# Mamba stage of a four-layer metaformer: step-size sum and kept columns off VectorE, a new order on four queues, and the conv taps in 8 transfers a pair instead of 18

## The chip, the cores and the metric

One core of a Trainium2 chip runs the whole program in one launch. The metric is the device time of that launch in microseconds. TensorE (PE) multiplies, VectorE (DVE), ScalarE (ACT) and GpSimd (POOL) work on elements, and SyncE (SP) issues the DMAs of this phase. Sixteen DMA engines move the data.

## What is computed

Sixteen images of 24 channels and 56 x 56 pixels go through four layers, each a mixer and a quantized feed-forward network, both with a residual. The change is in the mixer of the second layer alone, a Mamba block. Cut to what matters (`conv2d` is a 3 x 3 depthwise convolution, `conv1d` a causal one of three taps):

```python
xz = in_proj(x)                    # 48 channels to the conv branch, 48 to a gate
u = silu(conv2d(xz[:48]))          # sequence of 3136 pixels
xm, z = m_in_proj(u)               # 48 and 48
xm = silu(conv1d(xm) + b)
dt = softplus(dt_proj(x_proj(xm)[:3]) + dt_b)
B, C = x_proj(xm)[3:19], x_proj(xm)[19:35]
h = exp(dt * A) * h + (dt * xm) * B      # 16 states for each of 48 channels, pixel after pixel
y = sum(h * C) + xm * D
out = out_proj(m_out_proj(y * silu(z)) * silu(xz[48:]))
```

## The kernel before, in words

The phase is `mamba_phase`. The 3136 pixels are cut into 7 *stages* of MT = 448 pixels (8 image rows). There are two kinds of work, in one program order on every engine.

*Items.* An item is one pair of images in one stage; there are 56. Its front end, for item `j + 11` (`front`), multiplies nine shifted copies of the normalized image, the taps, with the folded input and conv weights: `project` (L1248), four matrix products from two tiles, `taps_5` (five taps of 24 channels, 120 partitions) and `taps_4` (96 partitions). `gate_image` (L1353, L1354) applies SiLU. For item `j + 10` (`inner`) follow `convolve` (L1257), `project_z`, `activate_inner` (`xm`), `activate_z` (`zs`), `project_dt`, `project_bc` and the softplus: `step_logs` on ScalarE (L1372 to L1384), `clip` on GpSimd (L1585), `quadratic` on ScalarE (L1395, L1398), `series` on GpSimd (L1590, L1592), and the sum `step_size` on VectorE (L1537). Its results `xm`, `zs`, `dt`, `gs`, `bcs` go to DRAM. The back end of item `j - 10` (`r`) loads `yt` and `gt`, multiplies (L1280), gates on GpSimd (L1597), multiplies (L1287) and stores `res`.

*Steps.* A stage has 6 passes (8 channels of all 16 images on 128 partitions), a pass 8 steps, a step two of the 16 states; 336 steps in all. In step `t` ScalarE makes two decays (`decay`, L1417, two steps ahead, three buffers), VectorE two products (`drive`, L1500) and two scans along the 448 pixels (`scan`, L1513) into one of 8 rows of `h`, GpSimd weighs both rows with `cs` (`weigh`, L1570), and TensorE adds them up in PSUM (`accumulate`, L1301). Once a pass there are `make_u` (L1489) and `times_z` (L1529) on VectorE. Every second step `save` (L1523) copies the last column of four rows of `h` to `kept`, from which the scans of the next stage, 48 steps on, start.

Every queue runs the loop `for j in range(-11, 67)`, `for k in range(6)`, so one item's work is spread over the six slots of six steps (t = 6j + k), each at a slot written by hand, and every engine waits on semaphores in that order. Eleven items pass before the first step: this is the prologue.

SP issues all transfers in that order too. `load_taps(j + 12)` at k = 0 issues 9 taps for each of two images into one of two buffers. `keep_rows` (L1121) stores 48 partitions into a DRAM tensor with dimensions 6 x 8 x 448, `store_bc` (L1143) 64 partitions into `bc_d[2q:2q+2, s]`, two images. At the border of a stage `load_bc(s, g)` (L1167) fills `bs` and `cs` for the next one, with each image repeated on 8 partitions: 8 transfers of 128 x 1792 x 4 bytes. They are issued at steps 48s - 5, - 3, - 1 and + 1, g = 3 right after the taps of that slot. The two sides of a tap transfer are:

```python
tile[m % 2][i][C * row:C * row + C, :]        # 24 partitions x 464
normed[2 * q + i, :, at:at + TAP_N]           # 24 channels x 464
```

Of the kernel before, what the change touches and what calls it, by code (L numbers as in the profile page):

```python
# [12 lines left out]
ALU = mybir.AluOpType  # L13
# [5 lines left out]
C = 24  # L19
# [966 lines left out]
def mamba_phase(nc, w, x, normed, mixed):  # L986
# [4 lines left out]
    with ExitStack() as ctx:  # L991
# [80 lines left out]
         squared, quads, taken, decays) = (buf.sem(n) for n in (  # L1072
             "silu_a", "silu_b", "silu_m", "silu_z", "absed", "relued", "exped", "excess", "lned",
             "bc_copied", "yi_copied", "squared", "quads", "taken", "decays"))
# [16 lines left out]
        with nc.Block() as block:  # L1091
            @block.sync
            def _(sp):
# [106 lines left out]
                for j in range(FIRST, LAST):  # L1200
                    front, inner, r = item(j + LEAD), item(j + LEAD - 1), item(j - LAG)
                    previous, r_done = item(j + LEAD - 2), item(j - LAG - 1)
                    for k in range(6):
# [15 lines left out]
                        if k == 3 and previous is not None:  # L1219
                            store_dt(previous)  # L1220
# [12 lines left out]
            def _(pe):  # L1233
# [71 lines left out]
                for j in range(FIRST, LAST):  # L1305
                    front, inner, r = item(j + LEAD), item(j + LEAD - 1), item(j - LAG)
                    for k in range(6):
                        t = 6 * j + k - 1
                        if k == 0 and front is not None:
                            reached(pe, silu_a, front)  # L1310
                            reached(pe, silu_z, done(front - 1))
                            reached(pe, yi_copied, done(j - LAG))
                            project(front, 0)
                        if k == 1 and front is not None:
                            reached(pe, silu_b, front)
                            reached(pe, relued, done(front - 1))
                            project(front, 1)
# [6 lines left out]
                        if k == 3 and inner is not None:  # L1324
                            reached(pe, taken, done(j - LAG))
                            convolve(inner)
                            project_z(inner)
                        if k == 4 and inner is not None:
                            project_dt(inner)
                            project_bc(inner)  # L1330
                        if k == 4 and r is not None:
                            out_inner(r, j + LEAD - 1)

            @block.scalar
            def _(act):
# [49 lines left out]

                def copy_bc(m):
# [32 lines left out]

                for j in range(FIRST, LAST):  # L1420
                    front, inner, r = item(j + LEAD), item(j + LEAD - 1), item(j - LAG)
                    for k in range(6):
# [3 lines left out]
                        if k == 2 and item(j - LAG - 1) is not None:  # L1426
                            take_result(j - LAG - 1)
# [15 lines left out]
                        if k == 5 and inner is not None:  # L1443
                            quadratic(inner)

            @block.vector
            def _(dve):
# [55 lines left out]
                def scan(t, i):  # L1503
# [12 lines left out]

                def save(t):

                    p, pair = divmod(t, 8)
                    at = p % DB * STATES + 2 * pair - 2  # L1520
                    row = (2 * t - 2) % 8
                    dve.wait_ge(scanned, 2 * t + 2)
                    dve.tensor_copy(kept[:, at:at + 4], h[:, row:row + 4, MT - 1]  # L1523
                                    ).then_inc(saved, 1)
# [15 lines left out]
                for j in range(FIRST, LAST):  # L1540
                    previous = item(j + LEAD - 2)
                    for k in range(6):
                        t = 6 * j + k
                        if 0 <= t < STEPS:
                            if t % 8 == 0:
                                make_u(t // 8)
                            drive(t, 0)
                            drive(t, 1)
                        if t % 2 == 0 and 0 < t <= STEPS:
                            save(t - 1)  # L1550
                        if t % 8 == 3 and 0 <= t // 8 - 1 < PASSES:
                            times_z(t // 8 - 1)
                        if k == 2 and previous is not None:
                            step_size(previous)
                        if 0 <= t < STEPS:
                            scan(t, 0)
                            scan(t, 1)

            @block.gpsimd
            def _(pool):  # L1560
# [26 lines left out]
                def series(m):  # L1587

                    pool.wait_ge(quads, m + 1)
                    pool.tensor_tensor(es[:], quad[:], es[:], ALU.mult).then_inc(sers, 1)  # L1590
                    pool.wait_ge(sers, m + 1)
                    pool.tensor_tensor(es[:], es[:], rv[:], ALU.add).then_inc(summed, 1)  # L1592

# [5 lines left out]
                for j in range(FIRST, LAST):  # L1599
                    inner, previous = item(j + LEAD - 1), item(j + LEAD - 2)  # L1600
                    for k in range(6):
# [3 lines left out]
                        if k == 0 and previous is not None:  # L1605
                            series(previous)
                        if k == 0 and item(j - LAG - 1) is not None:
                            times_gate(j - LAG - 1)
                        if k == 1 and inner is not None:
                            carry(inner)  # L1610
                        if k == 4 and inner is not None:
# [641 lines left out]
```

## Time and profile before

| | |
|---|---|
| median of 3 runs | 4461.85 us (4460.77 to 4468.82) |
| profiled execution | 4458.26 us, its span 4456.6 us |
| granted TensorE clock, mean | 0.931 |
| Mamba phase in the span | 1030 to 2656 us |
| first and last scan | 1204.0 and 2598.9 us |

The profile is one execution. A row of instructions names the line of the kernel, the engine, the operation, the tile written and the tiles read, how often it ran, its busy time and the mean duration of one. Short overlaps of neighbouring instructions are counted twice in busy sums of a group, not in those of an engine.

### The profile page before, as it was taken

How to read it: one execution, taken by the hardware profiler on the slowest of the kernel's cores; microseconds unless marked ns; L12 is line 12 of the kernel's file. 1: busy time of each engine (PE TensorE's matmuls, PEld its weight loads, DVE VectorE, ACT ScalarE, POOL GpSimd, SP SyncE). 2: the span in 40 equal slices, each digit the busy share in tenths (PEclk: the TensorE clock that was granted, in tenths of full speed). 3: DMA queues.
4: the chain of work that ended last, by engine and by line, in shares of the span. 5: the costliest groups of instructions: out<-in, count | busy, mean ns of one | idle time of the engine just before them, and what ended most of it. 6: DMA issues, size and time to landing. Idle time of an engine off the chain costs nothing. (4 is left out here: it accounts for less than half of the span.)

```text
span 4456.6 us, 73149 instructions
## 1 busy us (share of the span) xinstructions
PE 3640.5 (82%) x20680; PEld 2121.9 (48%) x20680; DVE 2888.3 (65%) x4570; ACT 2692.4 (60%) x4664; POOL 1600.1 (36%) x1447
## 2 busy tenths in 40 slices
PE   4899999785677888888876658689999786799956
PEld 2788888442233333333332214344444332799932
DVE  2666666671289989898999937566666665111146
ACT  4555555695666767676765328677777576233346
POOL 0333333101366767676766630045555400000000
PEclk9999999897889989999999979899999988899979
DMA  3000000123536364646544122100000022100012
GB/s 92 19 15 14 14 14 14 35 57 99 152 102 162 116 177 116 172 125 166 152 135 129 52 69 50 39 16 15 15 15 15 9 53 71 34 11 11 11 44 53
DMA packets 203144, 296.59 MB, mean 67 GB/s; under 512 B 68686, under 2 KB 188670, under 8 KB 202242
## 3 DMA queue, kind: packets, MB, share of 16 engines
q1 hardware_dynamic: 193798, 285.57, 24.4%
q10 hardware_dynamic: 9216, 9.65, 0.9%
q8 instruction: 37, 0.61, 0.1%
q14 instruction: 93, 0.76, 0.1%
HBM read 193.01 MB, written 102.03 MB: 66 GB/s over the span
## 5 line engine op out<-in xcount | busy, mean ns | idle before, releaser
L1570 POOL TENSOR_TENSOR mam_hc<-mam_h,mam_cs 128x896 f32<-128x896 f32 x336 | 712.5, 2126 | 333.4 <-DVE mam_h L1513 317.3
L1301 PE MATMUL mam_ps_y<-mam_hc,mam_ident 128*128 128x448 f32 x1344 | 628.4, 595 | 211.0 <-POOL mam_hc L1570 211.0
L1513 DVE TENSOR_TENSOR_SCAN mam_h<-mam_a,mam_kept,mam_dbx 128x448 f32<-128x448 f32 x672 | 729.3, 1123 | 1.2 <-ACT mam_a L1417 1.2
L1417 ACT ACTIVATE mam_a<-mam_ft,mam_a_neg 128x448 f32<-128x448 f32 x672 | 402.1, 656 | 242.4 <-DVE mam_h L1513 241.8
L1944 POOL TENSOR_TENSOR scan_ch<-scan_h,scan_cs 128x392 f32<-128x392 f32 x256 | 344.2, 1360 | 560.8 <-DVE scan_h L1910 560.8
L1301 PEld LDWEIGHTS mam_ps_y<-mam_hc,mam_ident 128*128 128x128 f32 x1344 | 261.3, 204 | 550.0 <-POOL mam_hc L1570 330.7
L1500 DVE TENSOR_TENSOR mam_dbx<-mam_ps_u,mam_bs 128x448 f32<-128x448 f32 x672 | 381.8, 611 | 92.5 <-DMA mam_cs<-dram_bc 91.1
L756 POOL TENSOR_TENSOR att_prob<-att_prob,att_share 128x588 f32<-128x588 f32 x128 | 151.9, 1186 | 452.1 <-DVE att_share L941 452.1
L1910 DVE TENSOR_TENSOR_SCAN scan_h<-scan_turned_in,scan_start 128x392 f32<-128x392 f32 x192 | 256.6, 1356 | 25.6 <-ACT scan_turned_in L1829 24.2
L1784 PE MATMUL scan_ps_merged<-scan_ch,scan_w_merge 128*128 128x392 f32 x512 | 230.6, 532 | 47.8 <-POOL scan_ch L1944 46.0
L2034 PE MATMUL lstm_ps<-lstm_hs,lstm_w_h 128*128 (+1 forms) x1344 | 264.9, 352 | 0.0
L2034 PEld LDWEIGHTS lstm_ps<-lstm_hs,lstm_w_h 128*128 128x128 f32 x1344 | 253.1, 188 | 3.0
L2084 DVE TENSOR_TENSOR lstm_kept<-lstm_gates,lstm_cell 128x224 f32<-128x224 f32 x56 | 22.0, 392 | 347.3 <-ACT lstm_gates L2055 347.3
L408 PE MATMUL f_xc_ff<-all_x,f_centre 128*128 (+1 forms) x256 | 128.3, 585 | 145.2 <-DVE all_x L298 145.2
L2025 PE MATMUL lstm_ps<-lstm_xs,lstm_w_x 128*128 (+1 forms) x896 | 181.4, 354 | 57.7 <-DMA lstm_xs<-in_rl_ones 57.7
L1784 PE MATMUL scan_ps_gate<-scan_ch,scan_w_merge 128*128 128x392 f32 x512 | 211.0, 494 | 0.0
L369 ACT ACTIVATE f_h<-f_hid 96x784 f16<-96x784 f32 x256 | 207.0, 811 | 0.0
L876 ACT ACTIVATE att_pt<-att_ps_t 128x512 f32<-128x512 f32 x128 | 76.4, 597 | 210.0 <-PE att_ps_t L817 210.0
L857 ACT ACTIVATE att_keys<-att_ps_keys 24x392 f32<-24x392 f32 x384 | 186.7, 486 | 22.8 <-PE att_ps_keys L785 19.8
L1772 PE MATMUL scan_ps_in<-scan_xin,scan_w_in 128*128 128x392 f32 x512 | 184.8, 505 | 17.6 <-DVE scan_ub L1919 15.4
L2025 PEld LDWEIGHTS lstm_ps<-lstm_xs,lstm_w_x 128*128 128x128 f32 x896 | 169.6, 189 | 61.1 <-issue 58.9
L1248 PE MATMUL mam_ps_a<-mam_taps,mam_win 120*128 120x448 f32 x224 | 121.9, 675 | 93.6 <-ACT mam_yi L1403 84.4
(215 smaller groups left out, 7984.1 us busy)
## 6 DMA issues: line engine op xcount, KB each, us to landing
mam_taps<-normed SPq DMA_DIRECT2D x1008, 43.5 KB
mam_bs<-dram_bc SPq DMA_DIRECT2D x28, 896.0 KB, 11.6
mam_cs<-dram_bc SPq DMA_DIRECT2D x28, 896.0 KB, 16.9
mam_ft<-dram_steps SPq DMA_DIRECT2D x42, 448.0 KB, 5.1
normed<-f_staged SPq DMA_DIRECT2D x384, 38.1 KB
f_mixed<-mixed SPq DMA_DIRECT2D x384, 36.8 KB
dram_gs<-mam_gs SPq DMA_DIRECT2D x56, 224.0 KB, 2.7
mam_gt<-dram_gs SPq DMA_DIRECT2D x56, 224.0 KB
```

The costliest lines, as they stand in the source:

```text
L369: act.activation(h16[:, 2 * a:2 * a + 2, :], hid[a][0:HID, :, 0:N], ACT.Copy).then_inc(ff["hidden16"], 1)
L857: o = act.activation(keys[p][0:C, :, h * T:(h + 1) * T], ps_keys[32 * h:32 * h + C, 0:N].rearrange("c (w t) -> c w t", w=WINS), ACT.Copy)
L1301: mm = pe.matmul(ps_y[p % 2][:, 0:MT], ident[:], hc[t % 2][:, i, :], start=False, stop=(t % 8 == 7 and i == 1))
L1417: act.activation(a[t % 3][:, i, :], ft[p % 2][:, 0, :], ACT.Exp, scale=a_neg[:, at:at + 1]).then_inc(decays, 1)
L1500: dve.tensor_tensor(dbx[:, i, 0:MT], ps_u[:, 0:MT], bs[:, 2 * pair + i, :], ALU.mult).then_inc(driven, 1)
L1513: dve.tensor_tensor_scan(h[:, n % 8, :], a[t % 3][:, i, :], dbx[:, i, 0:MT], kept[:, at:at + 1], ALU.mult, ALU.add).then_inc(scanned, 1)
L1570: pool.tensor_tensor(hc[t % 2][:], h[:, row:row + 2, :], cs[:, 2 * pair:2 * pair + 2, :], ALU.mult).then_inc(weighed, 1)
L1784: mm = pe.matmul(ps[:, 0:N], w_merge[:, a, n, :], ch[p][:, n, :], start=(n == 0), stop=(n == DIRS - 1))
L1910: dve.tensor_tensor_scan(out, a, v, start[p][:, n:n + 1], ALU.mult, ALU.add).then_inc(scanned, 1)
L1944: pool.tensor_tensor(out, hd, in_order(cs, 1 - half, d, t, p), ALU.mult).then_inc(weighed, 1)
L2025: pe.matmul(ps[p][:, q, 0:W], w_x[:, tap, q, :], xs[:, :, bass.ds(y + 1, 1), tap:tap + SIDE].rearrange("c j o q -> c j (o q)"), start=(tap ...
L2034: mm = pe.matmul(ps[p][:, q, 0:W], w_h[:, tap, q, :], hs[:, :, bass.ds(y, 1), tap:tap + SIDE].rearrange("c j o q -> c j (o q)"), start=Fal ...
```

## The change

- `step_size` leaves VectorE: ScalarE adds `log_b` to `ln1` (`shift_log`, Identity with a bias) and GpSimd adds `es`.
- GpSimd's series is spread: `series` at k = 1, `add_positive` at k = 2, `step_size` at k = 3 of the next item, `carry` now for `front` at k = 4, `clip` at k = 5, `times_gate` at k = 5 of the same item. `quadratic` moves on ScalarE from k = 5 to k = 1 of the next item, `take_result` from k = 2 to k = 3, and on SP `store_dt` from k = 3 to k = 4.
- `save` goes to ScalarE, behind the decays.
- On TensorE `convolve` and `project_z` come ahead of `accumulate` at k = 3, `project` behind it at k = 1 and k = 2.
- VectorE's loop is over steps alone, with `make_u` and `times_z` between the two scans of a step.
- The taps of an image come in 4 transfers of 3, 2, 1 and 3 taps, 8 a pair instead of 18.

```diff
-                        for tap in range(TAPS_5 + TAPS_4):
-                            at = (8 * s + tap // 3) * PAD + tap % 3
-                            tile, row = ((taps_5, tap) if tap < TAPS_5
-                                         else (taps_4, tap - TAPS_5))
-                            sp.dma_start(tile[m % 2][i][C * row:C * row + C, :],
-                                         normed[2 * q + i, :, at:at + TAP_N]
+                        for tile, row, dy, dx, n in ((taps_5, 0, 0, 0, 3), (taps_5, 3, 1, 0, 2),
+                                                     (taps_4, 0, 1, 2, 1), (taps_4, 1, 2, 0, 3)):
+                            shifted = bass.AP(
+                                tensor=normed.tensor,
+                                offset=(2 * q + i) * C * PADDED + (8 * s + dy) * PAD + dx,
+                                ap=[[1, n], [PADDED, C], [1, TAP_N]])
+                            sp.dma_start(tile[m % 2][i][C * row:C * (row + n), :], shifted
                                          ).then_inc(taps_in[m % 2], 16)
...
-                        pe.wait_ge(taps_in[m % 2], 288 * (m // 2 + 1))
+                        pe.wait_ge(taps_in[m % 2], 128 * (m // 2 + 1))
...
+                def shift_log(m):
+                    act.wait_ge(lned, m + 1)
+                    act.activation(ln1[:], ln1[:], ACT.Identity, bias=log_b).then_inc(shifted, 1)
...
+                def save(t):
+
+                    p, pair = divmod(t, 8)
+                    at = p % DB * STATES + 2 * pair - 2
+                    row = (2 * t - 2) % 8
+                    act.wait_ge(scanned, 2 * t + 2)
+                    act.activation(kept[:, at:at + 4], h[:, row:row + 4, MT - 1], ACT.Copy
+                                   ).then_inc(saved, 1)
...
+                        if t % 2 == 0 and 0 <= t - 3 < STEPS:
+                            save(t - 3)
+                        if k == 1 and previous is not None:
+                            quadratic(previous)
...
-                            reached(dve, saved, (t - 48) // 2 + 1)
+                            reached(dve, saved, t // 2 - 1)
...
-                def step_size(m):
-
-                    dve.wait_ge(lned, m + 1)
-                    dve.wait_ge(summed, m + 1)
-                    reached(dve, dt_out, 32 * m)
-                    dve.scalar_tensor_tensor(dt[:], ln1[:], log_b, es[:], ALU.add, ALU.add
-                                             ).then_inc(dts, 1)
...
+                make_u(0)
+                for t in range(STEPS + 4):
+                    p = t // 8
+                    if t < STEPS:
+                        drive(t, 0)
+                        drive(t, 1)
+                        scan(t, 0)
+                    if t % 8 == 7 and p + 1 < PASSES:
+                        make_u(p + 1)
+                    if t % 8 == 3 and p > 0:
+                        times_z(p - 1)
+                    if t < STEPS:
+                        scan(t, 1)
...
+                def step_size(m):
+                    pool.wait_ge(shifted, m + 1)
+                    pool.wait_ge(summed, m + 1)
+                    reached(pool, dt_out, 32 * m)
+                    pool.tensor_tensor(dt[:], ln1[:], es[:], ALU.add).then_inc(dts, 1)
```

## Rows read from the trace of the kernel before

**Rows 1.** Engines in the prologue and five of seven stages: busy us (instructions), clock, DMA

```profile
core 0: us, PE busy (x) PEld busy (x) DVE busy (x) ACT busy (x) POOL busy (x), PEclk, DMA share, GB/s
1030.00:1204.00 174.00, 113.60 (x222) 46.82 (x222) 10.68 (x25) 112.57 (x174) 40.31 (x48) 0.80 0.46 121
1204.00:1411.20 207.20, 155.61 (x352) 68.41 (x353) 188.76 (x236) 133.41 (x216) 131.35 (x87) 0.91 0.47 128
1411.20:1608.60 197.40, 165.10 (x386) 72.14 (x384) 188.77 (x238) 142.44 (x235) 139.20 (x94) 0.94 0.53 146
...
2013.10:2217.00 203.90, 172.40 (x397) 75.43 (x396) 184.88 (x237) 144.71 (x241) 143.20 (x97) 0.92 0.55 150
2217.00:2419.40 202.40, 153.69 (x350) 64.84 (x348) 188.46 (x237) 128.66 (x214) 140.43 (x90) 0.93 0.50 137
2419.40:2605.00 185.60, 114.19 (x243) 43.21 (x244) 181.27 (x227) 63.22 (x107) 111.26 (x58) 0.94 0.22 64
```

**Rows 2.** Groups of VectorE, 1200 to 2605 us

```profile
L1513 DVE TENSOR_TENSOR_SCAN mam_h<-mam_a,mam_kept,mam_dbx 128x448 f32<-128x448 f32 x672 | 729.3, 1123 | 1.2 <-ACT mam_a L1417 1.2
L1500 DVE TENSOR_TENSOR mam_dbx<-mam_ps_u,mam_bs 128x448 f32<-128x448 f32 x672 | 381.8, 611 | 92.5 <-DMA mam_cs<-dram_bc 91.1
L1523 DVE COPY mam_kept<-mam_h 128x4 f32<-128x4 f32 x168 | 136.8, 814 | 0.0
L1537 DVE SCALAR_TENSOR_TENSOR mam_dt<-mam_ln,mam_consts,mam_es 128x448 f32<-128x448 f32 x47 | 73.2, 1558 | 15.2 <-issue 13.5
```

**Rows 3.** Waits of VectorE, 1204 to 2600 us

```profile
DVE mam_dbx L1500 <- DMA mam_cs<-dram_bc: 74.3, 15, 12.0
```

**Rows 4.** The line of the copies: shortest, median, longest in ns

```profile
L1523 DVE COPY mam_kept<-mam_h x168: 148/992/1943, 1211.8 to 2600.1; 128x4 f32<-128x4 f32 x168
```

**Rows 5.** Groups of ScalarE and GpSimd nearest to the added work

```profile
L1341 ACT ACTIVATE mam_consts<-mam_consts 128x1 f32<-128x1 f32 x1 | 0.3, 278 | 0.0
...
L1398 ACT ACTIVATE mam_quad<-mam_quad,mam_consts 128x448 f32<-128x448 f32 x47 | 31.4, 668 | 1.5
...
L1592 POOL TENSOR_TENSOR mam_es<-mam_es,mam_rv 128x448 f32<-128x448 f32 x47 | 55.5, 1180 | 3.7
```

**Rows 6.** SP's issues in the prologue: start, duration, count

```profile
1064.94 0.57 SPq L1143 DMA_DIRECT2D dram_bc<-mam_bcs  x1
...
1133.15 7.32 SPq L1113 DMA_DIRECT2D mam_taps<-normed  x18
...
1188.92 0.55 SPq L1143 DMA_DIRECT2D dram_bc<-mam_bcs  x1
```

**Rows 7.** DMA, one store of `bcs`: 2375.9 to 2379.5 us whole, then 2377.5 to 2379

```profile
DMA packets 66, 0.11 MB, mean 32 GB/s; under 512 B 2, under 2 KB 66, under 8 KB 66
...
DMA packets 40, 0.07 MB, mean 48 GB/s; under 512 B 0, under 2 KB 40, under 8 KB 40
...
q1 hardware_dynamic: 40, 0.07, 12.9%
```

**Rows 8.** DMA, stores of `xm`, `zs`: 1068.5 to 1071.5, then 2368.5 to 2371 us

```profile
DMA packets 229, 0.37 MB, mean 122 GB/s; under 512 B 24, under 2 KB 229, under 8 KB 229
...
q1 hardware_dynamic: 229, 0.37, 35.7%
...
DMA packets 171, 0.27 MB, mean 110 GB/s; under 512 B 18, under 2 KB 171, under 8 KB 171
...
q1 hardware_dynamic: 171, 0.27, 35.8%
```

**Rows 9.** DMA with nothing but taps in flight, 1040 to 1044 us

```profile
DMA packets 352, 0.43 MB, mean 108 GB/s; under 512 B 120, under 2 KB 352, under 8 KB 352
```

**Rows 10.** DMA over the border before stage 3, 1793.7 to 1845.5 us

```profile
DMA packets 3924, 11.75 MB, mean 227 GB/s; under 512 B 598, under 2 KB 2769, under 8 KB 3921
...
q1 hardware_dynamic: 3921, 11.72, 90.5%
```

More of the change, by code:

```diff
@@ L1071, in mamba_phase @@
         (silu_a, silu_b, silu_m, silu_z, absed, relued, exped, excess, lned, bc_copied, yi_copied,
-         squared, quads, taken, decays) = (buf.sem(n) for n in (
+         squared, quads, taken, decays, shifted) = (buf.sem(n) for n in (
              "silu_a", "silu_b", "silu_m", "silu_z", "absed", "relued", "exped", "excess", "lned",
-             "bc_copied", "yi_copied", "squared", "quads", "taken", "decays"))
+             "bc_copied", "yi_copied", "squared", "quads", "taken", "decays", "shifted"))
         driven, scanned, u_made, zed, dts, saved = (buf.sem(n) for n in (
@@ L1218, in _ @@
                             load_gated(j - LAG + 1)
-                        if k == 3 and previous is not None:
+                        if k == 4 and previous is not None:
                             store_dt(previous)
@@ L1308, in _ @@
                         t = 6 * j + k - 1
[L1309 to L1317, printed above, removed]
+                        if k == 3 and inner is not None:
+                            reached(pe, taken, done(j - LAG))
+                            convolve(inner)
+                            project_z(inner)
                         if 0 <= t < STEPS:
@@ L1323, in _ @@
                             out_outer(j - LAG - 1, j + LEAD - 1)
[L1324 to L1327, printed above, removed]
+                        if k == 1 and front is not None:
+                            reached(pe, silu_a, front)
+                            reached(pe, silu_z, done(front - 1))
+                            reached(pe, yi_copied, done(j - LAG))
+                            project(front, 0)
+                        if k == 2 and front is not None:
+                            reached(pe, silu_b, front)
+                            reached(pe, relued, done(front - 1))
+                            project(front, 1)
                         if k == 4 and inner is not None:
@@ L1425, in _ @@
                             decay(t)
-                        if k == 2 and item(j - LAG - 1) is not None:
+                        if t % 2 == 0 and 0 <= t - 3 < STEPS:
+                            save(t - 3)
+                        if k == 1 and previous is not None:
+                            quadratic(previous)
+                        if k == 3 and item(j - LAG - 1) is not None:
                             take_result(j - LAG - 1)
@@ L1443, in _ @@
                         if k == 5 and inner is not None:
-                            quadratic(inner)
+                            shift_log(inner)
             @block.vector
@@ L1515, in scan @@
                                            ).then_inc(scanned, 1)
[L1517 to L1524, printed above, removed]
                 def times_z(p):
@@ L1530, in times_z @@
                                       ).then_inc(zed, 1)
-                def step_size(m):
-                    dve.wait_ge(lned, m + 1)
-                    dve.wait_ge(summed, m + 1)
-                    reached(dve, dt_out, 32 * m)
-                    dve.scalar_tensor_tensor(dt[:], ln1[:], log_b, es[:], ALU.add, ALU.add
-                                             ).then_inc(dts, 1)
[L1540 to L1557, printed above, removed]
+                make_u(0)
[11 more added lines that the diff above has]
+                        scan(t, 1)
             @block.gpsimd
@@ L1599, in _ @@
                 for j in range(FIRST, LAST):
-                    inner, previous = item(j + LEAD - 1), item(j + LEAD - 2)
+                    front, inner = item(j + LEAD), item(j + LEAD - 1)
+                    previous, r = item(j + LEAD - 2), item(j - LAG)
                     for k in range(6):
@@ L1604, in _ @@
                             weigh(t)
-                        if k == 0 and previous is not None:
+                        if k == 1 and previous is not None:
                             series(previous)
[L1607 to L1611, printed above, removed]
+                        if k == 2 and previous is not None:
+                            add_positive(previous)
+                        if k == 3 and previous is not None:
+                            step_size(previous)
+                        if k == 4 and front is not None:
+                            carry(front)
+                        if k == 5 and r is not None:
+                            times_gate(r)
+                        if k == 5 and inner is not None:
                             clip(inner)
```

2 lines of the change are left out of this document (added).

## The prediction

> **What bounds the kernel now.** I read the engine shares by stage first, then the groups of VectorE, then the waits, then single stretches of the DMA queues. The Mamba phase runs from 1030 to 2656 us of the 4456.6 us span; nothing outside it is touched. Its scan has 7 stages of 48 steps. In a middle stage of about 202 us VectorE is busy 185 us, ScalarE 145, GpSimd 143; TensorE shows 172 but its ends are modelled [rows 1]. VectorE's idle time is nearly all one wait: 74.3 us in 15 waits for the broadcast loads of `bs` and `cs` at the stage borders [rows 3]. So each middle stage is VectorE's work plus some 12 to 15 us of waiting for DMA. The last stage has no front-end work and takes 185.6 us, the prologue 174 us [rows 1]. Within VectorE's work the reader is to see two groups that don't belong to the recurrence: 168 copies of four columns at 0.81 us each and the step-size sums at 1.56 us [rows 2].
>
> **What the change takes off VectorE.** The copies last from 148 to 1943 ns with a median of 992 [rows 4]; a copy of four columns that takes a microsecond is waiting for something, and the shortest shows what it costs when it isn't. Removed: 24 a stage. At the mean that is 24 x 0.81 = 19.5 us, in the last stage, which has no other gap, nearer the median, 24 us. The step-size sum goes too: 8 x 1.56 = 12.5 us a stage. VectorE's stage falls from 185 to about 153 us; `make_u` moved between two scans hides at most 6 x 0.1 us more. The waiting columns have no other reader than the scan 48 steps later.
>
> **What it puts elsewhere.** ScalarE gets 24 copies a stage. The trace has no four-column copy there; the one-column activation took 0.28 us [rows 5], the smallest above nothing is my lower bound, and 0.67 us of a full-width one the upper; I take 0.28, so 6.7 us. `shift_log` is a full Identity, 0.67 us [rows 5], 5.3 us a stage. ScalarE: 145 + 12 = 157 us a stage. GpSimd gets one full add, 1.18 us [rows 5], and no other work: 143 + 9 = 152. The moved `series`, `clip`, `carry` and `times_gate`, and the new order on TensorE and ScalarE, issue the same instructions; behind each new wait on GpSimd stands the next `weigh`, which has `h`'s four steps of room before VectorE feels it. Of the new order I take nothing as gain or loss: after it VectorE, ScalarE and GpSimd all stand at 152 to 157 us. If that were all, a middle stage would need some 157 us plus a border wait of 15 or more, plus something for three queues that are nearly full, 180 us in all.
>
> **The taps.** Their 18 transfers a pair (SP issues them in 7.3 us [rows 6]) become 8, with the same rows and bytes. What changes is their shape, and the trace lets one read what shape does. A store of `bcs` (64 partitions, in DRAM two images) is 66 packets, 64 rows and 2 small ones, which I read as one completion for each DMA engine that takes part; in its middle it keeps 12.9% of 16 engines busy, two engines, with 40 rows in 1.5 us [rows 7]. Stores of `xm` and `zs` (48 partitions, in DRAM a slowest dimension of 6) hold 36% of 16 engines, six, and four of them in a row, with a `dt` pair before them, queue up for 3 us without taking more, so they all use the same six [rows 8]. The present taps (24 rows on both sides) have 120 small packets for 232 rows, one for two rows, 12 engines [rows 9]. All three fit one reading: the largest number up to 16 that divides the slowest dimension of both sides. The new transfers have a slowest DRAM dimension of 3, 2, (24) and 3: 3, 2, 12 and 3 engines.
>
> The Trainium skill, "DMA: Bandwidth & Descriptors", section on why a DMA increments its semaphore by 16, gives that same rule and adds that the lowest-numbered engines are the ones used. The rows agree as far as they reach; by this page the sum is the one I make below, without it and with the transfers spread as widely as now, it would be the first rival's.
>
> So I count the rows of the first engine for one item (two images). Now: taps 18 x 2 = 36. Then: 2 x (24 + 24 + 2 + 24) = 148, or 153 rows of the usual 1792 bytes. Beside them `bcs` 32, `xm`, `zs`, `dt` 6 x 8 = 48, `yt` 16, `gs` and `gt` 16, results 4, and three quarters of a pass's `ft` (8 double rows), `zy` and `ys`, 22: 138. Together 291 instead of 175. A row costs 0.077 us where two engines run through one long transfer (12.9% x 16 x 1.5 us / 40 [rows 7]) and 17.1 / 205 = 0.084 or 14.3 / 153 = 0.093 us where short transfers follow each other [rows 8]. The taps are long runs, the rest short: I take 0.079, hence 23.0 us an item, 184 us a stage. The border adds 8 broadcast loads of 0.917 MB, 0.459 MB for each engine; the rate of a whole border, 227 GB/s over 16 engines [rows 10], makes that 32 us, of which the first engine's share is all that counts. Sum 216 us for a full stage, against 201.5 now: **the first two DMA engines become the bound, above VectorE's 153.** With today's 175 rows it is 143 us, hidden. SP gains nothing from fewer issues, as it waits behind the full queue of that engine, and so do the transfers behind it.
>
> **The sum**, against the profiled execution of 4458.3 us (span 4456.6; the median of the runs, 4461.85, is 3.6 above it):
> - Prologue: 241 rows an item (no `yt`, `gt`, results, passes), 19.0 us, against a spacing of 15.5 us (first to ninth `bcs` store, 124 us in 8 [rows 6]): 3.5 x 11 items, and the first broadcast loads behind a fuller queue, together +40.
> - Stage 0: no output rows yet (263 an item), and three of four loads fell before it: 166 + 8 = 174, against 207.2: -33 [rows 1].
> - Stages 1 to 4: 4 x (216 - 201.5) = +58 [rows 1].
> - Stage 5: taps for half the items; first half bound by DMA (about 107), second half by VectorE (80): 187 against 202.4: -15.
> - Stage 6: only the copies: -24.
> - The tail of 51 us: same instructions, 0.
>
> Total +26: 4484, and 4488 against the median of the runs. I forecast **4488 us**, 0.6% slower, with an own range of 4450 to 4540.
>
> **The rivals.**
> *The taps stay spread* (12 engines or more, because the hand-built pattern is carried with 24 or 72 as its slowest dimension). Nothing in the trace shows a hand-built pattern. Then six stages come to 180 us each: 1215 - 1080 = 135, and the last 24: 4300 us. Chance 0.13.
> *The split holds but is cheap.* Rows at 0.075 us, as 20 rows in 1.5 us on one engine give, and the broadcast share at 26 us as the other engines leave room: 291 x 0.075 x 8 + 26 = 201 us in stages 1 to 4, -4 there; prologue +29, stage 0 -40, stage 5 -25, stage 6 -24, together -64: 4398 us against the runs' median, faster. It decides from a stage cost below about 209 us. For it speaks that queued rows run back to back; against it that in the border stretch the 16 engines were already 90.5% busy [rows 10] and every row was dearer. Chance 0.25.
> *Main case*, chance 0.45.
> *The split holds and is dear.* At 0.093 us a row, a full stage is 217 + 32 = 249 us: +190 in four stages, +76 in the prologue, stages 0 and 5 about as now, -24 in the last: about 4700; halfway to it from the main case, 4594. Chance 0.17.
> A rival on the compute side, that ScalarE's decays come late because the table-switching block, the logs and the copies follow each other (ScalarE at 157 us a stage), would cost only where the DMA bound is absent; it is in the 180 us of the first rival.
>
> **How the numbers follow.** About 0.2% (9 us) is what a measurement of this kernel can tell from no change. Faster: the first two rivals nearly whole, 0.36. Same: the low end of the main case, 0.10. Slower: 0.54. The range runs from 4310, which still takes in the upper half of the first rival, to 4600, which takes in a third of the dear case; it leaves out some 0.18.
>
> **What would show each step.** In the profile after: no DVE line for the kept columns or the step size, and ScalarE copies near 0.3 us; 8 tap transfers whose window shows about one small packet for every 20 rows and a DMA share near 3 of 16; VectorE idle in every middle stage, waiting for DMA or for decays behind late taps, not only at the borders; TensorE waiting for taps; SP's tap issues as long in total as 7 us although they are 8. Stage 6 at about 161 us whatever else happens, the prologue near 214 us. The prediction is wrong if the taps' small packets are as many as now, or if the first engine's rows run below 0.077 us.

## The result and the profile after

The changed kernel takes 4552.07 us (median of 4 runs, 4545.82 to 4555.38), the kernel before 4465.34 us (median of 4, 4460.77 to 4468.94): a ratio of 1.0197, 95% interval 1.0185 to 1.021. It is 2% slower. The direction came out as forecast and the time lies in the wide range of 4310 to 4600, but above the own range of 4450 to 4540. By the two spans (4553.7 and 4456.6) the loss is 97 us, and by the medians 87, not 26.

Where it lies, by the start of each stage's first scan in the two traces, in us:

| | before | after | difference | forecast |
|---|---|---|---|---|
| first scan | 1204.0 | 1239.4 | +35.4 | +40 |
| stage 0 | 207.2 | 191.0 | -16.2 | -33 |
| stages 1 to 4 | 805.8 | 903.2 | +97.4 | +58 |
| stage 5 | 202.4 | 208.9 | +6.5 | -15 |
| stage 6, to the last scan | 179.5 | 161.0 | -18.5 | -24 |
| behind the last scan | 1857.7 | 1850.2 | -7.5 | 0 |

The stretch behind the last scan runs from 1850.2 to 1862.5 us in the traces of the thirteen kernels of this document; why it differs was not looked into.

The engines by stage after, as [rows 1] has them for before (stages 2 and 3 are left out):

```profile
core 0: us, PE busy (x) PEld busy (x) DVE busy (x) ACT busy (x) POOL busy (x), PEclk, DMA share, GB/s
1030.00:1239.40 209.40, 116.74 (x214) 48.56 (x214) 5.00 (x16) 117.68 (x182) 47.99 (x59) 0.75 0.34 106
1239.40:1430.40 191.00, 148.98 (x364) 67.52 (x364) 160.00 (x203) 145.94 (x256) 140.53 (x96) 0.92 0.45 137
1430.40:1647.30 216.90, 168.88 (x386) 74.21 (x386) 161.76 (x206) 151.22 (x267) 146.21 (x102) 0.87 0.45 132
...
2106.40:2333.50 227.10, 174.86 (x395) 75.20 (x396) 159.98 (x205) 151.97 (x271) 147.16 (x103) 0.86 0.44 129
2333.50:2542.40 208.90, 151.96 (x344) 64.09 (x342) 159.63 (x205) 132.52 (x240) 141.67 (x94) 0.89 0.42 122
2542.40:2710.00 167.60, 114.00 (x244) 42.99 (x244) 156.64 (x203) 66.44 (x133) 110.71 (x58) 0.93 0.31 82
```

The offload did what it says: VectorE's busy time falls from about 187 to 160 us a stage, ScalarE and GpSimd rise to 152 and 147. But a middle stage takes 217 to 230 us, so VectorE is idle for 55 to 70 us of it. The granted clock of TensorE is lower too, 0.86 to 0.87 in stages 1 to 4 where the kernel before had 0.92 to 0.94 in the stages shown [rows 1]. The groups of VectorE and the line of the copies, now on ScalarE, show what it waits for (beside [rows 2] and [rows 4]):

```profile
L1532 DVE TENSOR_TENSOR_SCAN mam_h<-mam_a,mam_kept,mam_dbx 128x448 f32<-128x448 f32 x672 | 738.3, 1129 | 153.7 <-ACT mam_kept L1431 120.3
...
L1519 DVE TENSOR_TENSOR mam_dbx<-mam_ps_u,mam_bs 128x448 f32<-128x448 f32 x672 | 381.5, 611 | 220.7 <-DMA mam_cs<-dram_bc 163.3
```

```profile
L1431 ACT ACTIVATE mam_kept<-mam_h x168: 190/192/208, 1245.9 to 2704.5; 128x4 f32<-128x4 f32 x168
...
  DVE mam_h L1532: 120.3, 25
```

```profile
DVE mam_dbx L1519 <- issue: 57.3, 5, 12.7
```

A copy takes ScalarE 192 ns, where it took VectorE 992 in the median. Two idle times have grown. The first is the wait for the broadcast loads: it went from 91.1 us [rows 2] to 163.3, and ahead of the first product of stages 1 to 5 another 57.3 us were added, where the same view of the kernel before has none. The profile names no releaser for these ("issue"); by the program VectorE waits there for the first pair of `bs` and `cs`. The second is new and costs 120.3 us in 25 scans: the copy on ScalarE, though short, arrives late. The scan of an even step writes over the rows of `h` of four steps before, which the copy has to read first, and in the changed kernel it waits for that (`reached(dve, saved, t // 2 - 1)`). From VectorE's timeline, one gap at a border and three of the five within stage 3, which come once in every six steps; four turns from 1966.95 to 2072.66 make 26.4 us each:

```profile
1918.63 1.16 DVE L1519 TENSOR_TENSOR mam_dbx<-mam_ps_u,mam_bs 128x448 f32<-128x448 f32 x2 [17.59 <-DMA mam_cs<-dram_bc]
...
1966.95 2.19 DVE L1532 TENSOR_TENSOR_SCAN mam_h<-mam_a,mam_kept,mam_dbx 128x448 f32<-128x448 f32 x2 [5.21 <-ACT mam_kept L1431]
...
1993.70 2.18 DVE L1532 TENSOR_TENSOR_SCAN mam_h<-mam_a,mam_kept,mam_dbx 128x448 f32<-128x448 f32 x2 [5.79 <-ACT mam_kept L1431]
...
2072.66 2.19 DVE L1532 TENSOR_TENSOR_SCAN mam_h<-mam_a,mam_kept,mam_dbx 128x448 f32<-128x448 f32 x2 [5.33 <-ACT mam_kept L1431]
```

The taps have the shape that was forecast. From 1040 to 1044 us only they move:

```profile
DMA packets 173, 0.30 MB, mean 75 GB/s; under 512 B 11, under 2 KB 173, under 8 KB 173
...
q1 hardware_dynamic: 173, 0.30, 19.7%
```

11 small packets to 162 rows (before, 120 to 232 [rows 9]) and 19.7% of 16 engines, 3.15 engines; at 4 us x 3.15 / 162 a row takes 0.078 us. The waits of TensorE in the prologue name them too:

```profile
PE mam_ps_a L1249 <- DMA mam_taps<-normed: 65.6, 10, 11.9
```

### The profile page after: what moved, and what is told of

It reads as the page before. It is cut to its first block and busy times, and to the rows that moved or that the text cites. A ratio compares the mean times of both kernels' runs of the same rounds, so it can differ in the third digit from the quotient of the medians.

```text
span 4553.7 us, 72669 instructions
## 1 busy us (share of the span) xinstructions
PE 3640.9 (80%) x20680; PEld 2120.2 (47%) x20680; DVE 2690.1 (59%) x4346; ACT 2750.1 (60%) x4888; POOL 1645.8 (36%) x1503
## 5 line engine op out<-in xcount | busy, mean ns | idle before, releaser
L1567 POOL TENSOR_TENSOR mam_hc<-mam_h,mam_cs 128x896 f32<-128x896 f32 x336 | 698.6, 2083 | 372.5 <-DVE mam_h L1532 219.7
L1532 DVE TENSOR_TENSOR_SCAN mam_h<-mam_a,mam_kept,mam_dbx 128x448 f32<-128x448 f32 x672 | 738.3, 1129 | 153.7 <-ACT mam_kept L1431 120.3
L1519 DVE TENSOR_TENSOR mam_dbx<-mam_ps_u,mam_bs 128x448 f32<-128x448 f32 x672 | 381.5, 611 | 220.7 <-DMA mam_cs<-dram_bc 163.3
L1781 PE MATMUL scan_ps_in<-scan_xin,scan_w_in 128*128 128x392 f32 x512 | 183.9, 503 | 17.1 <-DVE scan_ub L1928 14.9
L827 PE MATMUL att_ps_out<-att_pt,att_vals 128*24 128x49 f32 x2048 | 189.5, 208 | 2.1 <-ACT att_pt L876 2.1
```

The lines of the kernel that those rows point to most:

```text
L827: pe.matmul(ps_out[0:C, cols], vals[p][:, win, 0:C], pt[p][:, q, 64 * half:64 * half + T], start=True, stop=False)
L1519: dve.tensor_tensor(dbx[:, i, 0:MT], ps_u[:, 0:MT], bs[:, 2 * pair + i, :], ALU.mult).then_inc(driven, 1)
L1532: dve.tensor_tensor_scan(h[:, n % 8, :], a[t % 3][:, i, :], dbx[:, i, 0:MT], kept[:, at:at + 1], ALU.mult, ALU.add).then_inc(scanned, 1)
L1567: pool.tensor_tensor(hc[t % 2][:], h[:, row:row + 2, :], cs[:, 2 * pair:2 * pair + 2, :], ALU.mult).then_inc(weighed, 1)
```

## The experiments

Two changes were under suspicion, the taps and the new order, so both were undone alone and together, and the taps also put alone into the kernel before. The ratios are all to the kernel before, run beside (4460.7, 4462.3 and 4459.9 us in the three groups of runs).

**a_taps18**: the changed kernel with the old taps.

```diff
-  for tile, row, dy, dx, n in (... 4 transfers an image)
+  for tap in range(TAPS_5 + TAPS_4):        # 9 transfers an image, as before
...
-  pe.wait_ge(taps_in[m % 2], 128 * (m // 2 + 1))
+  pe.wait_ge(taps_in[m % 2], 288 * (m // 2 + 1))
```

> The changed kernel with the taps in 18 transfers a pair again, all else as changed. Theory A (the first two DMA engines, loaded by the narrow tap transfers, set the pace of the middle stages): the stages fall from 228 to about 180 us and the time to about 4300 us. Theory B (a wait ring between the queues sets it: GpSimd's gate product now waits for ScalarE's copy ahead of the next weighing, so TensorE's sums and its projections come late, and with them ScalarE's block and the decays; the narrow taps cost only the prologue and the stage borders): the item period of 25.6 us stays, the prologue gives back 35 us and the borders some 6 x 7 us, about 4475 us.

**b_taps8**: the kernel before with the new taps, the same edit the other way round.

> The kernel before with nothing changed but the taps in 8 transfers. Theory A: middle stages at 216 us or more, prologue +35, about 4580 us. Theory B: prologue +35 us, borders + 6 x 7 us, no stall between borders, about 4540 us.

**a_gate0**: the changed kernel with `times_gate` one slot later on GpSimd.

```diff
   weigh(t)
+  if k == 0 and item(j - LAG - 1) is not None:
+      times_gate(j - LAG - 1)
...
-  if k == 5 and r is not None:
-      times_gate(r)
```

> The changed kernel with GpSimd's gate product (times_gate) back at k = 0 of the next item, behind the weighing; the 8 narrow tap transfers stay. Theory A: no change, 4540 to 4560 us. Theory B: the stall of some 5 us an item goes in stages 1 to 5 until the next limit, the first DMA engine at 22 us an item: about 4450 us, down to 4380 if that engine has room.

**a_taps18_gate0**: both edits.

> Both together: 18 tap transfers and the gate product back at k = 0. Both theories: about 4300 us, as neither the narrow transfers nor the ring is left. If the ring has another cause (TensorE's new order, or the copies on ScalarE), 4420 us or more.

Measured:

| | us | ratio, 95% |
|---|---|---|
| a_taps18 | 4450.32 | 0.9975, 0.9964 to 0.9985 |
| b_taps8 | 4557.81 | 1.0211, 1.0194 to 1.0228 |
| a_gate0 | 4446.94 | 0.9968, 0.9953 to 0.9983 |
| a_taps18_gate0 | 4317.43 | 0.9677, 0.966 to 0.9693 |

So there are two separate costs, each somewhat dearer where the other is gone. The narrow taps cost 102 us in the changed kernel, 97 in the kernel before and 130 once the gate is mended. The gate's place costs 105 us with the narrow taps and 133 without. The taps alone cost the kernel before about as much as the whole change did, and with both undone the rest of the change is worth 143 us. For b_taps8 the result lies between what the two theories gave, so it does not choose between them by itself. a_gate0 does, at 4447 where theory A had 4540 to 4560 and B 4450, and so does a_taps18, at 4450 where A had 4300 and B 4475.

*The first cost, read in the traces.* VectorE's gaps over 1.7 us around the start of stage 3, to beyond its middle, in a_gate0:

```profile
1833.69 1.16 DVE L1519 TENSOR_TENSOR mam_dbx<-mam_ps_u,mam_bs 128x448 f32<-128x448 f32 x2 [17.43 <-issue]
...
1845.62 1.17 DVE L1519 TENSOR_TENSOR mam_dbx<-mam_ps_u,mam_bs 128x448 f32<-128x448 f32 x2 [5.55 <-DMA mam_cs<-dram_bc]
...
1877.20 1.16 DVE L1519 TENSOR_TENSOR mam_dbx<-mam_ps_u,mam_bs 128x448 f32<-128x448 f32 x2 [18.39 <-DMA mam_cs<-dram_bc]
```

and in a_taps18_gate0:

```profile
1744.17 1.17 DVE L1518 TENSOR_TENSOR mam_dbx<-mam_ps_u,mam_bs 128x448 f32<-128x448 f32 x2 [7.01 <-issue]
...
1755.93 1.17 DVE L1518 TENSOR_TENSOR mam_dbx<-mam_ps_u,mam_bs 128x448 f32<-128x448 f32 x2 [5.38 <-DMA mam_cs<-dram_bc]
...
1782.56 1.17 DVE L1518 TENSOR_TENSOR mam_dbx<-mam_ps_u,mam_bs 128x448 f32<-128x448 f32 x2 [11.98 <-DMA mam_cs<-dram_bc]
```

Until the next border no gap is longer than 1.7 us in either: between the borders the first DMA engines keep up. The difference is at the border, 41.4 us of gaps against 24.4. Most of it, 10.4 us, is in the first gap, ahead of the stage's first product, and 6.4 in the last one. Over the five borders of stages 1 to 5 the first gaps are, in a_gate0 and in a_taps18_gate0:

```profile
DVE mam_dbx L1519 <- issue: 85.1, 5, 21.1
```

```profile
DVE mam_dbx L1518 <- issue: 30.7, 5, 7.0
```

while VectorE's later waits for `cs` are 133.4 and 103.6 us. So of some 84 us, 54 come ahead of the first product and 30 behind. In the changed kernel, which the ring slows, the first gaps are 57.3 us: part of this cost is hidden there. The first pair of loads is issued right behind 8 tap transfers and a store of `bcs`. At the border of stage 3 VectorE goes on 20.9 us after its issue in a_gate0 (1812.81 to 1833.69), and 13.2 us after it in a_taps18_gate0 (1730.96 to 1744.17). An estimate fits this: the first engines have 148 rows of taps ahead of the loads instead of 36, which at 0.079 us a row is 8.8 us. No trace here tells the single engines apart, so this is a reading.

For the last gap, SP's timeline of the changed kernel shows one part (start, duration of the issues):

```profile
2111.53 12.74 SPq L1115 DMA_DIRECT2D mam_taps<-normed  x8
...
2128.27 0.58 SPq L1168 DMA_DIRECT2D mam_bs<-dram_bc  x1
2128.89 0.59 SPq L1168 DMA_DIRECT2D mam_cs<-dram_bc  x1
```

Eight tap issues hold SP for 12.7 us behind the broadcast loads, and the last pair of loads, for which VectorE waits, can't be issued until they are out. That alone isn't what narrowness costs: in a_taps18_gate0 the 18 issues at the same place hold SP about as long, and the pair follows at 1765.57.

```profile
1751.22 13.17 SPq L1113 DMA_DIRECT2D mam_taps<-normed  x18
```

At the border of stage 3 the pair is issued 18.9 us after the start of the tap issues in a_gate0 and 14.4 us in a_taps18_gate0, as the transfers between them are held too. The busy digits of the DMA between 1868 and 1925 us, a border of the changed kernel in 40 slices, show that the other engines run dry meanwhile: nearly all 16 busy, then one to three tenths of them, then all again.

```profile
DMA  9999999999963331211121119999999984353221
```

**a_wide_gate0**: a_gate0 with the same 8 transfers, but the DRAM side walked with the 24 channels as its slowest dimension. The rows of a tile stand in another order by this, and the weights' rows follow them on the host side of the layout.

```diff
-  ap=[[1, n], [PADDED, C], [1, TAP_N]])
+  ap=[[PADDED, C], [1, n], [1, TAP_N]])
```

> Still 8 tap transfers of the same bytes and the gate product at k = 0, but each transfer walks channel by channel, tap by tap (slowest dimension 24 on the DRAM side; the weights' rows are put in that order on the host), so that by the reading of the divisors each runs on 12 engines. If the narrowness costs: 4310 to 4325 us, as with 18 transfers, or a little less because SP issues less. If the number or the size of the transfers costs: 4447 us, as with the 8 narrow ones.

Measured 4287.05 us, 0.9622 (0.9598 to 0.9646): 160 us below the narrow form and 30 below the 18 transfers, more than the little that was expected; 20 of the 30 are in the first scan's time. From 1060 to 1140 us, in the prologue and before any broadcast load, the DMA line has for it, and then for a_gate0 and a_taps18_gate0:

```profile
DMA packets 7306, 11.47 MB, mean 143 GB/s; under 512 B 1032, under 2 KB 7302, under 8 KB 7302
```

```profile
DMA packets 4655, 7.70 MB, mean 96 GB/s; under 512 B 437, under 2 KB 4653, under 8 KB 4653
```

```profile
DMA packets 6949, 9.84 MB, mean 123 GB/s; under 512 B 1571, under 2 KB 6945, under 8 KB 6945
```

Its first scan is at 1171.4 us, theirs at 1238.6 and 1191.7. The number of transfers was not the fault, the order of the dimensions was. In these 80 us 2935, 1975 and 2496 tap rows of 1856 bytes moved, 432 to an item, so an item has about 151 small packets in the wide form, 96 in the narrow one and 272 with 18 transfers. The Trainium skill, "DMA: Bandwidth & Descriptors", section on why a DMA increments its semaphore by 16, ties the number of engines to the slowest dimension of both sides; by this rule the four transfers of an image use 3, 2, 12 and 3 engines in the narrow form and 12 each in the wide one. The trace agrees: that makes 40 and 96 small packets an item, 56 apart, where 55 are counted, and the narrow form's share was 19.7%.

**b_wide**: the kernel before with the 8 wide transfers.

> The kernel before with the taps in 8 wide transfers alone. Fewer issues shorten the prologue as in the changed kernel (20 us between 18 and 8 wide transfers) and the borders by some 2 us each: about 4430 us. If only the changed kernel has room for it, 4462 us.

Measured 4446.5 us, 0.9963 (0.9949 to 0.9977). There the wide taps alone give 13 us by the medians, less than half of what was expected (4430); in its profile the first scan comes 6.3 us earlier and the seven stages together take 10 us less. VectorE is busy for 186.8 of 201 us there (1876 to 2077 us), which leaves little to win.

**a_wide_gate0_bc_early**: the last pair of broadcast loads of a border issued one slot earlier, ahead of the taps.

```diff
-  if (t + 5) % 48 in (0, 2, 4, 6) and 0 <= (t + 5) // 48 < STAGES:
-      load_bc((t + 5) // 48, (t + 5) % 48 // 2)
+  if (t + 5) % 48 in (0, 2, 4, 5) and 0 <= (t + 5) // 48 < STAGES:
+      load_bc((t + 5) // 48, ((t + 5) % 48 + 1) // 2)
```

> As the wide transfers with the gate product at k = 0, and the last pair of broadcast loads of a border issued one step earlier, ahead of the taps. VectorE's longest wait of a border, 12 us before step 48s + 6, should shrink by about 3 us of taps in six stages: some 15 to 20 us less than the same without it. If the border is bound by bytes alone, no change.

Measured 4241.8 us, 0.9516 (0.9494 to 0.9537), the fastest of all and 45 us below a_wide_gate0, more than twice what I expected. Middle stages take 174.5 to 178.1 us instead of 183.5 to 186.8. Behind the first scan, VectorE's waits for `cs` fall from 100.2 to 51.1 us, which is as much as the whole gain. A stage of it:

```profile
1694.60:1872.70 178.10, 160.40 (x396) 70.99 (x395) 161.60 (x205) 151.20 (x272) 149.48 (x104) 0.97 0.59 169
```

**a_narrow_gate0_bc_early**: the same with the narrow taps, to see whether their cost at the border is only the place in SP's queue.

> 8 narrow tap transfers, the gate product at k = 0, and the last broadcast pair of a border issued ahead of the taps. Against the same without the last edit (4447 us). If the narrow transfers cost at the borders because the last broadcast pair queues behind 148 rows on the first engines, nearly all of that cost (20 us in each of 5 borders) goes, and the 45 us that the wide form gained from the same edit: about 4320 us. If the first engines' sum of rows over the border is what counts, the order of the queue can't help it: 4400 us, as in the wide form's gain alone.

Measured 4429.72 us, 0.9935 (0.9918 to 0.9951), only 17 below a_gate0. That is above both figures that were expected, so the queue's order is not all of it. SP's timeline at a border and the three longest waits of VectorE over all stages:

```profile
2035.22 2.24 SPq L1168 DMA_DIRECT2D mam_cs<-dram_bc  x1
2037.50 18.19 SPq L1115 DMA_DIRECT2D mam_taps<-normed  x8
```

```profile
DVE mam_dbx L1519 <- issue: 93.5, 5, 21.5
DVE mam_dbx L1519 <- DMA mam_cs<-dram_bc: 63.7, 21, 27.8
DVE mam_ps_u L1508 <- DMA mam_ft<-dram_steps: 42.8, 10, 8.2
```

The last pair is out ahead of the taps, and the wait for `cs` falls from 161.5 us in a_gate0 to 63.7, in both with some 28 us ahead of the first scan. But the taps now hold SP for 18 us, and 42.8 us of waiting for the load of `ft` behind them are new: part of the stall moves to the next transfer in the queue. And the longest wait, the one for the first pair of a stage, is one that this edit doesn't touch: 93.5 us here, 85.1 in a_gate0.

*The second cost, read in the trace.* One turn of it in the changed kernel, from its timeline:

```profile
1962.82 0.64 ACT L1362 ACTIVATE mam_xm<-mam_ps_c,mam_conv_b 128x448 f32<-128x448 f32 x1 [1.17 <-PE mam_ps_c L1258]
...
1964.13 1.28 ACT L77 ACT_TABLE_LOAD   x1
...
1965.43 1.23 ACT L1422 ACTIVATE mam_a<-mam_ft,mam_a_neg 128x448 f32<-128x448 f32 x2
...
1966.56 0.19 ACT L1431 ACTIVATE mam_kept<-mam_h 128x4 f32<-128x4 f32 x1
...
1971.81 0.52 ACT L1408 ACTIVATE mam_yi<-mam_ps_a 128x448 f32<-128x448 f32 x1
...
1972.41 1.14 POOL L1601 TENSOR_TENSOR mam_yi<-mam_yi,mam_gt 128x448 f32<-128x448 f32 x1 [2.72 <-ACT mam_yi L1408]
...
1975.04 4.12 POOL L1567 TENSOR_TENSOR mam_hc<-mam_h,mam_cs 128x896 f32<-128x896 f32 x2
...
1977.17 3.35 PE L1302 MATMUL mam_ps_y<-mam_hc,mam_ident 128*128 128x448 f32 x4 [4.27 <-POOL mam_hc L1567]
...
1982.14 2.12 PE L1249 MATMUL mam_ps_a<-mam_taps,mam_win 120*128 120x448 f32 x4
1982.25 0.54 ACT L1413 ACTIVATE mam_res<-mam_ps_c 64x448 f32<-64x448 f32 x1 [3.43 <-PE mam_ps_c L1288]
...
1987.31 0.54 ACT L1354 ACTIVATE mam_xg<-mam_ps_b 64x448 f32<-64x448 f32 x1 [1.92 <-PE mam_ps_b L1249]
...
1989.57 0.64 ACT L1362 ACTIVATE mam_xm<-mam_ps_c,mam_conv_b 128x448 f32<-128x448 f32 x1 [1.17 <-PE mam_ps_c L1258]
```

`copy_inner` (L1408) stands on ScalarE behind the logs. `times_gate` (L1601), now in the same slot on GpSimd, waits for it, and behind it stand `clip` and the weighings (L1567). TensorE's `accumulate` waits for these 4.27 us, and behind it now stand the output product and `project`. So ScalarE's result and gates come late, then `xm`; then follow the table load, the decays and the copy, which ends at 1966.75 in this turn and lets the scan go that had stood for 5.21 us. The logs and `copy_inner` of the next turn come behind these. It is a ring through four queues: each turn starts as late as the last one ended. In a_gate0 the name `mam_kept` is gone from VectorE's waits in this stage, and the gaps within the stage with it.

**a_taps18_pe_old**: if it is a ring, it can be cut at TensorE too, with `project` back ahead of `accumulate` and the gate left at k = 5.

```diff
+  if k == 0 and front is not None:    # ahead of accumulate, as before
+      ...
+      project(front, 0)
+  if k == 1 and front is not None:
+      ...
+      project(front, 1)
   if k == 3 and inner ...
...
-  # the same two blocks behind accumulate, at k == 1 and k == 2
```

> 18 tap transfers, the gate product left at k = 5 as changed, and only TensorE's two projections back ahead of the sums at k = 0 and 1. If the wait ring of the change closes over TensorE's new order (late weighing, so late sums, so late projections), it is cut here: about 4330 us. If it closes otherwise, over the gate product alone: 4450 us, as with 18 transfers alone.

Measured 4343.42 us, 0.9738 (0.9716 to 0.976): 107 below a_taps18, and VectorE's wait for the kept columns in its stage 3 falls from 28.0 us in 6 to 4.5 in 2:

```profile
DVE mam_h L1531 <- ACT mam_kept L1430: 28.0, 6, 6.4
```

```profile
DVE mam_h L1531 <- ACT mam_kept L1430: 4.5, 2, 2.8
```

The ring can be cut at either place, for 133 us at the gate product and 107 at the projections, so it takes both moves to close it. The mean product of `accumulate` took 605 ns in the changed kernel and 567 in a_gate0, and the granted clock over the stages was 0.88 and 0.92; how much of each turn is the clock was not taken apart.

**a_wide_gate0_bc_early_pe_old**: TensorE's old order in the fastest form, to see whether the new one is worth anything once the gate is mended.

> The best version so far (wide transfers, gate product at k = 0, early broadcast pair, 4242 us) with TensorE's projections back ahead of the sums. With the ring cut at the gate product already, TensorE's order should be worth nothing: 4235 to 4250 us. If the decays' remaining waits (7 us in all) hang on it, 4235.

Measured 4280.17 us, 0.9593 (0.9577 to 0.9609): 38 us slower, where no change was expected. Its waits in stage 3:

```profile
PE mam_ps_a L1249 <- ACT mam_yi L1408: 14.1, 8, 2.0
...
DVE mam_h L1532 <- ACT mam_a L1422: 6.2, 7, 1.6
...
DVE mam_h L1532 <- ACT mam_kept L1431: 3.5, 2, 2.8
```

With `project` first, TensorE waits 14.1 us a stage for the PSUM tile that `copy_inner` frees, ahead of `accumulate`. VectorE's waits for ScalarE are 9.7 us there and 0.9 in the fastest form, and the stage is 188.6 us against 178.1. That is a reading of the waits; no run took the wait for `copy_inner` away by itself.

**a_taps18_gate0_save_dve**: a_taps18_gate0 with the copies back on VectorE, between the products and the first scan of a step.

```diff
+  if t % 2 == 0 and 0 < t <= STEPS:
+      save(t - 1)                       # dve.tensor_copy, as before
...
-  if t % 2 == 0 and 0 <= t - 3 < STEPS:   # no longer on ScalarE
-      save(t - 3)
```

> 18 tap transfers, gate product at k = 0, and the copies of the kept columns back on VectorE, ahead of the scans. By the rows of the kernel before (0.81 us each, 24 in each of 7 stages) +137 us: about 4450 us; less, down to 4400, if half of them fall where VectorE waits anyway.

Measured 4427.26 us, 0.993 (0.9906 to 0.9953), 110 us slower; expected were 137.

```profile
L1530 DVE COPY mam_kept<-mam_h 128x4 f32<-128x4 f32 x168 | 183.6, 1093 | 0.0
```

They take 183.6 us there, more than before, and 110 us come out at the end; where the other 74 are covered was not looked into. So the copies on VectorE account for most of the 143 us. The step-size sum wasn't moved alone.

## Why the prediction was right, and where it was wrong

As a whole it was wrong: 26 us of loss were forecast and 97 measured by the spans. That the direction came out right was luck. It hangs on a term that the prediction put at nothing: without the ring (a_gate0) the kernel takes 4447 us, a little less than before.

**Right in the main: the work taken off VectorE.** The first rival's 4300 us is the change without its two costs, and a_taps18_gate0 took 4317. Part of that nearness is chance: its six stages took 1113 us where 1080 were forecast, its first scan came 12 us earlier, which nobody forecast, and stage 6 gave 22 us instead of 24. VectorE's stage came to 160 to 162 us, not 153: the busy time of the engine fell by 24 to 29 us a stage where the groups' sums gave 32. The busy sums of groups count overlaps of neighbours twice, and I subtracted them from a busy time that doesn't; that this is the whole of the difference I did not test. ScalarE's copy was 0.192 us against the 0.28 taken from the one-column activation [rows 5] and called a lower bound. Stage 6 fell by 18.5 us, near the mean of the copies (19.5) and not near the median (24).

**Right: the shape of the taps.** Three engines, 0.078 us a row against 0.079, from one store of `bcs` [rows 7] and the small packets [rows 9]. The prologue term followed from it within 5 us (+35.4 for +40).

**Wrong: "the first two DMA engines become the bound, above VectorE's 153", 216 us a middle stage.** With the taps narrow and no ring (a_gate0) stages 1 to 4 take 204.4 us each, and between the borders VectorE hardly waits. I added the rows of 8 items and the share of the broadcast loads as if the first engines worked through the stage without a pause. But 204.4 is below the 209 from which I had it turn out faster, and what the split costs is paid at one place, the border: the first pair of broadcast loads comes late (85.1 us of waiting against 30.7 over five borders), and so do the later ones (133.4 against 103.6 us behind the first products). The second rival's stage of 201 us is nearer, but not for its reason, as a row did not run at 0.075 us. In the four stages the split costs 66 us (817.5 in a_gate0, 751.3 in a_taps18_gate0), where my two figures for a stage, 216 with the bound and 180 without, gave 144. The term was 46 us too high (4 x 11.6).

**Wrong, and what sank the sum: "Of the new order I take nothing as gain or loss."** It costs 86 us in stages 1 to 4 (903.2 against 817.5) and 22 in stage 5, and 105 in all. I had the parts in hand. I named the `weigh` behind each new wait on GpSimd and gave it four steps of room in `h`, which is VectorE's room alone: `accumulate` waits for the weighing too, and the new order had just put TensorE's projections behind `accumulate`. And of the moved copies I wrote that the columns "have no other reader than the scan 48 steps later". That is so, but the rows they are read from are written again four steps on, and there VectorE waited for ScalarE: 120.3 us in 25 scans. I followed each moved wait one queue far, and not round to where it started. And I put ScalarE's late decays down as a rival that "would cost only where the DMA bound is absent"; since there was no such bound, it was there.

The sum missed by 71 us of the spans, and would have missed by more if two errors had not partly cancelled: stages 1 to 4 were over-charged 46 us for the split and under-charged 86 for the ring, which makes the 39 that are missing there; stage 5's 22 more is the ring's 22; stage 0's +17, which has no back-end items and so no ring, is mostly the split: it takes 192.4 in a_gate0 and 180.1 with 18 taps, against my 174. The remaining parts are -5 in the prologue, +6 in stage 6 and -8 behind the last scan.

**What I said would show.** The copies near 0.3 us, the small packets, 3 of 16 engines, TensorE waiting for taps, the prologue near 214 (209.4): seen. Stage 6 was to take about 161 us where [rows 1] has 185.6, up to 2605 us; to the same point, the end of the last `times_z` at about 2709, it took 167, 6 us more. VectorE idle in every middle stage and not only at the borders: seen, but for another reason, the ring. SP's tap issues as long as 7 us although they are 8: 5.5 to 8.7 within stage 3, 12.7 to 14.9 at the borders.

**Open.** How much of the broadcast pair's 45 us comes from its earlier landing and how much from the taps that no longer meet it; the cause of the 38 us for TensorE's order, which is read and not tested; why the first pair of loads takes longer behind narrow taps, for which the queue on the first engines is an estimate; and what the lower clock adds to the ring. No run issues the first pair ahead of the narrow taps, which would test the third.

## What to carry to other kernels

When waits move in hand-ordered queues, follow each moved wait from queue to queue until it comes back to its start or ends in an engine with slack: a wait put one slot too early here cost 5 us in every turn, and it took two moves together to close the ring. When a copy moves to another engine, ask not only who reads what it writes, but who next writes what it reads. Count a transfer's engines by the slowest dimension of both sides before merging transfers, and let the merged form keep a wide one; the same 8 transfers, walked in the other order of dimensions, took 160 us less. And where a few DMA engines are overloaded, look at what stands behind their transfers at the busiest moment, in the issuing queue and on those engines, rather than at their load on average.

## What the runs showed that I had not expected

- Eight narrow tap issues took SP 5.6 us between borders, 12.7 behind the broadcast loads, and 18.2 with one more pair ahead (a_narrow_gate0_bc_early). At the border shown of the changed kernel the busy share of the 16 engines was meanwhile at one to three tenths.
- A copy of 128 x 4 columns takes 0.192 us on ScalarE with hardly any spread (190 to 208 ns), and 1.093 us in the mean on VectorE with GpSimd busier than before (149.6 and 150.5 us in two stretches of 199 and 202 us of that run, against 143 a stage), where the kernel before had 0.814 [rows 2]. That the one comes from the other was not tested.
- Moving one pair of broadcast loads of 0.9 MB each ahead of 8 taps was worth 45 us over the phase with the wide taps, 17 with the narrow ones.
